# A fused attention and mixture-of-experts layer: weight loads, planning arithmetic and the last attention pair put in another order

## What is computed

```
# attention: 16 heads, 4 key/value heads, head dimension 32 + 32 (the second part rotated), values 64
remote = 1024 - 128                       # 14 blocks of 64 keys, each averaged to one key; 128 last keys stay
k2, v2 = concat(block means, last 128 keys)
scores = (q_sem @ k_sem2 + q_geo @ k_geo2) / sqrt(32) * exp(logit_scale); masked by k_pos <= pos
out    = softmax(scores) @ v2 @ Wo
# ffn: router over 16 experts, the best 4 for each row, weights normalised over these 4
act = silu(x @ gate[e]) * (x @ up[e]);  y[e] = act @ down[e]     # 256 -> 224 -> 256
out = sum over the 4 chosen e of weight * y[e]
```

## Time and profile before

| | |
|---|---|
| median of 3 runs | 378.23 us (376.97 to 378.33) |
| the profiled execution's own time | 376.97 us |
| its span, first to last instruction | 375.2 us |
| PE busy | 337.1 us, 90% of the span |
| DVE / ACT / POOL busy | 250.1 / 180.5 / 216.1 us |
| chain that ended last | PE 77%, DVE 13%, DMA 3%, ACT 3%, issue 2% |
| mean granted TensorE clock | 0.983 of full |

### The profile page before, as it was taken

How to read it: one execution, slowest core, us unless ns; L and a number is a source line. 1 busy time by engine, 2 the same in 40 slices (tenths; PEclk the granted TensorE clock), 3 DMA queues, 4 the chain that set the end, 5 groups by cost and what they waited for, 6 DMA issues and landing times.

```text
span 375.2 us, 8164 instructions
## 1 busy us (share of the span) xinstructions
PE 337.1 (90%) x2085; PEld 280.9 (75%) x2086; DVE 250.1 (67%) x799; ACT 180.5 (48%) x526; POOL 216.1 (58%) x200
## 2 busy tenths in 40 slices
PE   0399989988989999949999989999999999999990
PEld 0395666436666777837999989999999999999880
DVE  3889996898769888843788855555555555555450
ACT  1632176766013444232688845555555555555450
POOL 1510456466456576793566656666666666666564
PEclk9999999999999999996999999999999999999996
DMA  7995114423155634327998657776666666667544
GB/s 251 352 328 130 57 59 142 161 97 134 58 190 182 197 135 140 122 84 224 266 309 167 111 98 112 109 111 105 111 106 110 110 111 111 112 112 111 60 45 54
DMA packets 50097, 52.36 MB, mean 140 GB/s; under 512 B 5632, under 2 KB 47120, under 8 KB 50072
## 3 DMA queue, kind: packets, MB, share of 16 engines
q0 software_dynamic: 14640, 19.34, 30.4%
q1 hardware_dynamic: 35432, 32.73, 29.6%
HBM read 30.14 MB, written 21.91 MB: 139 GB/s over the span
## 4 chain that ended last, share of the span: by engine, by line
PE 77%; DVE 13%; DMA 3%; ACT 3%; issue 2%; SPq 1%; POOLq 1%; DVEq 0%; ACTq 0%
PE bank L1426 64%; PE bank L1769 5%; PE bank L1790 4%; PE bank L1523 2%; DVE lneg L1214 1%; DMA x_all<-in_L_attn_x 1%; DVE lex L1224 1%; ACT lex L862 1%; ACT x_all L788 1%; DMA out_rows<-y,idx 1%; DVE stats L991 1%; PE bank L1438 1%; DVE logit_left L1061 1%; SPq L647 1%; DMA xg<-xn_by_expert 1%
## 5 line engine op out<-in xcount | busy, mean ns | idle before, releaser
L766 POOL DMA_INDIRECT out_rows<-y,idx x79 | 123.2, 1559 | 76.1 <-ACT y L964 55.0
L737 POOL DMA_INDIRECT xn_by_expert<-x_all,slot_i x64 | 64.4, 1007 | 47.9 <-DMA xn_by_expert<-x_all,slot_i 29.0
L1404 DVE SCALAR_TENSOR_TENSOR act<-bank,xg,sg 128x224 f32<-128x224 f32 x79 | 35.6, 450 | 49.4 <-ACT sg L951 48.7
L1426 PE MATMUL bank<-wgu_hi,xh 128*128 x158 | 65.3, 413 | 1.0 <-DVE wdn_lo L1237 1.0
L1426 PE MATMUL bank<-wgu_lo,xh 128*128 x158 | 58.3, 369 | 0.0
L1426 PE MATMUL bank<-wgu_hi,xl 128*128 x158 | 57.8, 366 | 0.0
L951 ACT ACTIVATE sg<-bank 128x224 f32<-128x224 f32 x79 | 28.2, 357 | 57.9 <-PE bank L1426 57.9
L1396 DVE TENSOR_TENSOR xl<-bank,xh 128x256 fp32r<-128x256 f32 x79 | 33.5, 424 | 32.6 <-ACT xh L947 32.6
L1426 PE MATMUL bank<-wdn_hi,ah 112*128 x158 | 51.2, 324 | 0.8 <-issue 0.7
L1426 PE MATMUL bank<-wdn_hi,al 112*128 x158 | 44.6, 282 | 0.0
L1426 PE MATMUL bank<-wdn_lo,ah 112*128 x158 | 44.5, 281 | 0.0
(11 more groups left out here) (239 smaller groups left out, 641.6 us busy)
## 6 DMA issues: line engine op xcount, KB each, us to landing
xg<-xn_by_expert SPq DMA_DIRECT2D x79, 129.0 KB, 2.5
wgu<-in_L_ffn_gate_proj SPq DMA_DIRECT2D x16, 224.0 KB, 3.6
wgu<-in_L_ffn_up_proj SPq DMA_DIRECT2D x16, 224.0 KB, 4.2
wdn<-in_L_ffn_down_proj SPq DMA_DIRECT2D x16, 224.0 KB, 4.9
x_all<-in_L_attn_x SPq DMA_DIRECT2D x8, 256.0 KB, 4.9
xr<-in_L_attn_x SPq DMA_DIRECT2D x14, 128.0 KB, 2.4
out_rows<-xr SPq DMA_DIRECT2D x14, 128.0 KB, 1.8
out_rows<-y,idx POOLq DMA_INDIRECT x79, 3.8
```

Source lines behind the costliest of these rows:

```text
L737: gp.indirect_dma_start(xs_d, bass.IndirectOffsetOnAxis(slot_i[:, z, r:r + 1], 0), x_all[:, z, :], None).then_inc(xs_in[p], DMA)
L766: gp.indirect_dma_start(out_rows, bass.IndirectOffsetOnAxis(idx[r % RING][:, 0:1], 0), ysb[r % 4][:, :], None, compute_op=ALU.add).then_in ...
L1404: nc.vector.scalar_tensor_tensor(av[t.par][:, :], bank[2 + t.par][:, I:2 * I], xg[t.slot][:, D + 1:D + 2], sg[t.par][:, :], ALU.mult, ALU. ...
L1426: return nc.tensor.matmul(o, lhsT, rhs, start=start, stop=stop)
```

## The change

- SP: the wait for the zeroed rows (`scattered`) moves behind `tables_ready`. Experts 4 and 5 are no longer loaded ahead of the local stage. Experts 4 to 8 are loaded one at a time: 4 ahead of `store_sum(0)`, 5 to 8 behind `load_residual` of the loop round.
- SP at the seam: `tile_of` is no longer read ahead; all 8 task loads go first, then experts 9 and 10, then `store_sum(5)` and `store_sum(6)`.
- ACT: the rounding of experts 4 to 8 moves from pairs 1 to 5 to pairs 2 to 6.
- POOL: the low parts of experts 4 and 5 stand beside dispatch groups 12 to 15 (before: experts 4, 5 and the first part of 6 beside 11 to 15).
- DVE: `plan_tasks` ahead of the local stage; `weights(1)`, `bound_tasks`, `weights(2)`, `keep_tables`, `split_low(0)`, `split_low(1)`, `weights(3)`, `split_low(2)` beside units 0 to 7; `split_low(3)` behind the local stage; none in pair 0.
- PE and ACT: turning and keeping the probabilities of pair 6 moves into `step(-1)`, behind the turning of task 1; `attend` of pair 6 moves behind the gate/up product of task 0.
- `wv_s`, `wks`, `zero` and some small tiles lie elsewhere in SBUF.

```diff
-        SPREAD_AT, ASEM_AT = 3, 5
+        SPREAD_AT, ASEM_AT = 2, 5
-        SPLITS = ((), (4,), (5,), (6,), (7,), (8,), ())
+        SPLITS = ((), (), (4,), (5,), (6,), (7,), (8,))
+        LOADS = ((4, 9), (5, 10), (6, 11), (7, 12), (8, 13))
-        LOW_AT = 11
+        BETWEEN = (4, 5)
...
             load_residual(0)
-            sp.wait_ge(wv_done, 1)
-            for s in range(TRASH):
-                sp.wait_ge(scattered[s], DMA)
-            for k in (4, 5):
-                load_late(k)
...
             load_residual(REMOTE - 1)
-            load_between(6, 9)
-            load_between(7, 10)
+            load_between(0)
             for i in range(REMOTE - 3):
                 store_sum(i)
-                if i == 0:
-                    load_between(8, 11)
                 load_residual(i + 2)
-            for i in range(REMOTE - 3, REMOTE - 1):
-                store_sum(i)
+                load_between(i + 1)
+            store_sum(REMOTE - 3)
...
-            tiles = [tile_of(j) for j in range(RING // 2)]
             for p in range(GT):
                 sp.wait_ge(xs_in[p], K * GROUPS * DMA)
-            for j in range(RING // 2):
-                load_task(j, j, tiles[j])
+            for j in range(RING):
+                load_task(j, j)
             load_late(9)
-            for j in range(RING // 2, RING):
-                load_task(j, j)
-            store_sum(REMOTE - 1)
             load_late(10)
+            for i in range(REMOTE - 2, REMOTE):
+                store_sum(i)
...
-                if n >= LOW_AT:
-                    split_low(EARLY + (n - LOW_AT) // 2, (n - LOW_AT) % 2)
+                if r == K - 1:
+                    split_low(BETWEEN[q // 2], q % 2)
...
# ACT, step(j)
+                if j.counts is None and j.r == -1:
+                    for u in range(NB):
+                        p_keep(u, Pair(0, REMOTE - 1))
...
# PE, step(j): ahead of the gate/up product, and behind it
                 if j.counts is None and j.r == -1:
                     for u in range(NB):
-                        attend(u, Pair(0, REMOTE - 1))
+                        p_turn(u, Pair(0, REMOTE - 1))
...
+                if j.counts is None and j.r == -1:
+                    for u in range(NB):
+                        attend(u, Pair(0, REMOTE - 1))
```

More of the change, by code:

```diff
@@ L229, in build @@
         mean, var, dif, rstd, tmp, shift_x = (wa.take(n, [P, NT]) for n in ("mean", "var", "dif", "rstd", "tmp", "shift_x"))
+        zero = wa.take("zero", [P, D])
         x_keys = wa.take("x_keys", [P, DC, NB, NKEY])
@@ L233, in build @@
         k_mean = wa.take("k_mean", [NBLK, NB, KD])
+        logit = wa.take("logit", [P, NT, EX])
+        left = wa.take("logit_left", [P, NT, EX])
+        top = wa.take("top", [P, NT, 8])
         chosen = wa.take("chosen", [P, (NT + 1) * E], BF16)
@@ L236, in build @@
         ones_b = wa.take("ones_b", [P, P], BF16)
-        logit = wa.take("logit", [P, NT, EX])
-        left = wa.take("logit_left", [P, NT, EX])
-        top = wa.take("top", [P, NT, 8])
         ones = wa.take("ones", [P, P])
@@ L268, in build @@
         wqs = Region(oT_at[0], DC * H * DS * 4).take("wqs", [P, DC, H * DS])
[L269 to L272, removed]
+        wv_s = wa.take("wv_s", [P, DC, HKV * DV])
+        wks = wa.take("wks", [P, DC, KD])
         wo_s = wa.take("wo_s", [P, H // 2, D])
@@ L602, in load_late, with load_between @@
                     load_part(sp, k, part, w_late[next(n for n, ks in enumerate(LATE) if k in ks)])
-            def load_between(k, landed):
+            def load_between(n):
+                k, landed = LOADS[n]
                 for p in range(GT):
@@ L633, in _, with load_task @@
             sp.wait_ge(tables_ready, 1)
+            for s in range(TRASH):
+                sp.wait_ge(scattered[s], DMA)
             load_residual(1)
             load_residual(REMOTE - 1)
-            load_between(6, 9)
-            load_between(7, 10)
+            load_between(0)
             for i in range(REMOTE - 3):
                 store_sum(i)
-                if i == 0:
-                    load_between(8, 11)
                 load_residual(i + 2)
-            for i in range(REMOTE - 3, REMOTE - 1):
-                store_sum(i)
[L646 to L650, removed]
+                load_between(i + 1)
+            store_sum(REMOTE - 3)
+            def load_task(j, s):
+                tile = sp.value_load(td_i[0:1, ds(j, 1)], min_val=0, max_val=N * K // P - 1)
                 sp.dma_start(xg[s][:, :], xs_d[ds(tile * P, P), :]).then_inc(xg_in[s], DMA)
@@ L739, in _ @@
                     keep_weights(n + 1)
-                if n >= LOW_AT:
-                    split_low(EARLY + (n - LOW_AT) // 2, (n - LOW_AT) % 2)
+                if r == K - 1:
+                    split_low(BETWEEN[q // 2], q % 2)
                 for p in range(GT):
                     gp.wait_ge(xs_in[p], (n + 1) * DMA)
-            split_low(EARLY + (K * GROUPS - LOW_AT) // 2, 1)
-            with gp.Fori(EARLY + (K * GROUPS - LOW_AT) // 2 + 1, IN_LOOP) as e:
+            with gp.Fori(BETWEEN[-1] + 1, IN_LOOP) as e:
                 for part in range(2):
@@ L1184, in diagonals @@
                 last.then_inc(ready, 1)
+            plan_tasks()
             for n in range(REP_ON_ACT, 2 * HKV):
@@ L1275, in beside @@
                     diagonals(bd_g, rep_g, bdg_ready)
-                elif n == SPREAD_AT - 2:
-                    plan_tasks()
+                    weights(1)
                 elif n == SPREAD_AT - 1:
@@ L1285, in beside @@
                     weights(3)
-                elif n == 5:
-                    split_low(0)
+                elif n in (4, 5):
+                    split_low(n - 4)
                 elif n == 7:
-                    split_low(1)
+                    split_low(2)
             l_largest(0)
@@ L1379, in attention @@
                 probabilities(t)
-                if t.first:
-                    split_low(3)
             for u in range(NB):
                 rope(u, Pair(0, 0))
-            split_low(2)
+            split_low(3)
             keep_before()
@@ L1798, in _ @@
             expert(Tile(0, 0))
-            for u in range(NB):
-                p_turn(u, Pair(0, REMOTE - 1))
             for u in range(NB):
```

3 lines of the change are left out of this document (removed).

## The result

The changed kernel takes 382.34 us in the median of 5 runs (380.49 to 384.04), the kernel before 377.14 beside it (376.30 to 378.33): the ratio is 1.0134, with an interval of 1.009 to 1.0177. That is slower by 1.3%, and outside the range of 372.3 to 380.5. The profiled execution took 381.69 us, 4.72 more than the one of before (376.97); its span is 379.9 instead of 375.2.

The account below looks back on a forecast made before the run. PE bounds the kernel, with its only hole at the seam, 163.35 to 175.90 us. A 0.8 us seam gain, other terms netting nothing, turns 376.97 into 376.2; 376.5 given between that and the median's 377.4, range 372.3 to 380.5.

Parts of the forecast that it names:

- Stores behind weights: SP at the seam: pair 5's stores issue behind task loads and two experts; ACT stalls 0 to 1.5 us, costed at 0.
- the third rival: Stores decide: ACT waits 1.5 us, PE pays most, 377.2 us; chance 0.12, including SP reaching the dispatch wait late.
- The lead of ACT over PE: Expert loop's start: ACT runs more than a task ahead of PE's need, so its store stall costs 0.
- half clock: PE at the seam: the clock falls as before, lasting 5.4 us and costing 2.7 us.
- The seam: Between remote stage and expert loop: PE starts 2.1 us earlier, work to task 2's turning becomes 7.45 us; 0.8 us gained.
- the gap ahead of task 1: Seam: task 1's load lands 0.56 us later behind task 0's, for its own tile_of read.
- The end of the remote stage: PE ends it at about 163.95, 0.6 us later through DVE's local-stage order; cost nothing, as PE waits anyway.
- The dispatch: POOL's scatters ahead of the seam: -2.15 + 2 + 0.5 - 0.4 = 0, so xs_in stays at 164.05.
- the sign: Dispatch: the group after 62 us starts 7.2 us later, not 9.3, as experts 4 and 5 no longer load there.
- all late loads: Dispatch: loads of experts 5 to 8 may meet groups' last scatters, up to 2.5 us each; 2 us taken.
- The 0.5 us for DVE's splits: Dispatch: moved DVE splits lengthen POOL's scatter issues; 0.5 us taken, bounds 0 and 1.7.
- The late dispatch at 380.3: Rival: late weight loads and DVE's splits make the dispatch 4.15 us later, xs_in at 168.2; 380.3 us, chance 0.24.

Follow-up runs that it names:

- e9: Changed kernel with pair 5's stores ahead of the dispatch wait and pair 6's ahead of experts 9 and 10: 379.21 us, 1.0019 of the kernel before.
- e1: Changed kernel with the stores of pair 5 put back ahead of the wait for the dispatch: 381.28 us, 1.011 of the kernel before.
- e14: Kernel before with only the weights of experts 4 to 8 loaded, rounded and split late: 376.92 us, 0.9973.
- e13: Kernel before with DVE's new order alone: 380.11 us, 1.0064.
- e10: e9 with DVE's old order: 378.44 us, 1.0 of the kernel before.
- e4: Kernel before with its late stores moved behind the task loads and experts 9 and 10, all else left: 377.64 us, 1.0023.
- e12: e4 with expert 11 also loaded ahead of the stores of pairs 5 and 6: 381.22 us, 1.0089 of the kernel before.
- e2: Changed kernel with pair 5's stores behind the eight task loads but ahead of experts 9 and 10: 385.01 us, 1.0156 of the kernel before.
- e7: Kernel before with only the four tile_of reads moved, between the stores of pairs 4 and 5: 375.26 us, 0.9966.

## Why the prediction was wrong

- *What failed: the step "Stores behind weights".* It was costed at 0, with 1.5 us as the other end; measured by e9 it is about 4.3 us, and 3.36 idle + 1.75 of clock in the profile. The mechanism was named, there and as the third rival. Its terms one by one: The first store was put at 175.6 and went at 178.38: the dispatch released SP 2.1 us later (+1.94 at the first load), and eight loads took 8.07 us and not 7.4, because the step from one load to the next is 1.1 us. The prediction divided the 3.69 us of four loads by four, where three steps and one issue of 0.35 lie in them. The landing was put at 2 to 5 us from there; it was at 184.22, 5.8 us behind the first issue: 0.5 us to the second store, 5.34 for its landing. ACT's need was put at 179.1 and was at 179.69, nearly right. The lead of ACT over PE was put at more than a task (2.39 us) and was 1.2 us.
- *What it left out: the second waiter.* It said of POOL's scatter that it "has 53 us of idle time". The idle time of a whole loop says nothing of its start. Once the stores have landed, POOL reads its tables for 2.1 us before its first scatter, and the scatter landed 6.30 us later in e1. POOL must have scattered one of four output buffers before ACT's fifth copy, and e1 shows that the stores of pair 6 alone cost 3.30 us by that way.
- *The clock.* The stall in the loop was followed by 3.4 us at half clock (1.2 GHz), from 187.0 to about 190.4, which no term had. The prediction priced half clock only at the seam.
- *The seam was right in kind, wrong in two sizes.* One `tile_of`, no store, `p_turn` behind task 1, as the prediction said would be seen. PE began at 169.35 and not at 167.5, 1.85 late, as the dispatch was 2.09 late. Its work to the third turning took 6.12 and not 7.45 us: the clock was at half already at 167 to 168, when PE had no work to lose, and back at full at 173.3. From 169.35 on that is 4.0 us, 0.47 of them idle, so it cost 1.8 us and not 2.7. The rest of the difference is in `p_turn`, which added some 0.4 us (an estimate, from the sums at either clock) where 0.74 was taken, and in the gap ahead of task 1 (0.47, not 0.56). The gain was 0.28 instead of 0.8. With the seam 0.5 us short and the stores at 5.1, the forecast's 376.2 becomes 381.8, and the profiled execution took 381.69. The end of the remote stage was right in size, 169.35 - 5.32 = 164.03 where 163.95 was forecast, but partly by luck: PE also ran at 0.50 of full clock from 58 to 60 us, which no term of the local stage had.
- *The dispatch.* Its sum of 0 was 2.1 in the profile, inside its bounds; the terms were off in both directions. The group behind 62 us took 7.91 us (from 61.81 to 69.72), 1.4 less than before, where 2.15 were taken and 7.2 us were named as the sign. Up to 124.20 the dispatch was still 2.0 us ahead of the kernel before. Then the groups that start at 124.20, 133.40 and 142.39 took 9.20, 8.99 and 10.11 us, against 7.69, 7.44 and 9.07 for the same three before: 4.1 us, where 2 were taken for all late loads. It lies in the landing of each group's last scatter, 4.5, 4.2 and 4.0 us instead of 3.0, 2.6 and 3.0. e14, with late weights alone, has it too (10.70, 8.26 and 9.45 us for these groups). The 0.5 us for DVE's splits are not seen: over the whole dispatch lengthened issues lost 1.6 us, before 2.1. DVE's order costs 0.64% (2.4 us) by itself where experts 4 and 5 are loaded early (e13), and no more than some tenths of a per cent where they are not (e9 and e10). In time the late loads weigh little: e10 has them, with no cover ahead of its first load, and is at 1.0.
- *The rivals.* The late dispatch at 380.3 came nearest in time, for the wrong reason: in the changed kernel the last issue was 2.1 us late, and the third turning was not late at all. The chance of 0.12 for the stores was too low, and their price was capped by one waiter's lead.

## What to carry to other kernels

When transfers are moved back in a queue, list everyone who waits for them, and for each the time of its need, not the idle share of its engine; behind one waiter with little slack stands the next, through the number of its buffers. Late stores were nearly free at 176.1 and cost 3.4 us (0.9%) at 177.6: test such a move by pushing it one step further. And when a step leaves the path, the one that takes its place (here the dispatch) has had no reason to be on time.

## What the runs showed of the hardware

- A store's landing goes with what stands ahead of it on the same queue: 1.7 us with no weights in flight (the kernel before, at 163.2), 1.8 behind eight task loads (e9), 3.3 right behind one expert's weights (e4), 4.61 behind two (e12), 5.34 behind two in the changed kernel. The Trainium skill, page "DMA: Bandwidth & Descriptors", section "Queues, rings and completion order", says that each engine takes the descriptors of a queue in order; these numbers agree with that, but don't separate it from the load on all engines (DMA share 1.02).
- The clock fell with a stall of 3.36 us (changed kernel), of 3.39 (e2) and of 3.60 (e12), not with one of 3.30 (e1), whose windows show 1.00 throughout. In the changed kernel and in e12 it fell only when PE had been back at work for 1.2 to 1.3 us, in e2 some 0.6 us before PE was back (198:199 shows 0.70, PE resumes at 198.99). So a stall of about this size cost 3.3 us in one kernel and 5.1 in another; what tells them apart is open.
- One task load follows the other on SP after 1.1 us where each has its tile number read ahead of it, and after 0.5 us where four were read before (1.96 us for four loads in e7).
